# Two slots' value products in succession in a multi-head attention over 1024 tokens

## The chip, the cores and the metric
The kernel runs on one core of a Trainium2 chip. The metric is the device time in microseconds of one execution, as the median of several runs. One further execution was profiled; its rows give times in microseconds from the first instruction, durations of one instruction in nanoseconds in some views.

## The reference, cut to what matters
The program computes four layers on x (4 batches, 128 channels, 32 x 32 positions): two convolution-like blocks (a one-head attention, then a multi-head attention at three scales, fused), then two transformer layers on the 1024 tokens of each batch (causal one-head attention and 16 routed experts; 8-head attention with a bias and 8 experts). The change touches the 8-head attentions with 1024 tokens, of which there are two: scale 1 of the second block, and the attention of the last layer.

```python
attn = jnp.einsum('bhdn,bhdm->bhnm', q, k) / HEAD_DIM ** 0.5     # HEADS = 8, HEAD_DIM = 16
attn = jax.nn.softmax(attn, axis=-1)
out = jnp.einsum('bhnm,bhdm->bhdn', attn, v)
...
scores = jnp.einsum('bihd,bjhd->bhij', q, k) / jnp.sqrt(jnp.asarray(hd, x.dtype))
scores = scores + col_bias[None, :, None, :]
attn = jax.nn.softmax(scores, axis=-1)
out = jnp.einsum('bhij,bjhd->bihd', attn, v).reshape(B, N, D)
```

## The kernel before, in words
`many_heads_attention` is called for 1024, 256, 64 tokens (heads0, heads1, heads2) and once more for 1024 (heads3). The flag `whole` is true for 256 and 64 tokens. For 1024 tokens each of the 4 batches has 32 slots (`SLOTS`). A slot stands for one tile of 128 keys, against 512 queries, in 4 heads. Eight slots (`T`) make a chunk, two chunks (`NH`) make a half (4 of the 8 heads), two halves a batch. The first batch is written out, the others run in a loop whose body is the 32 slots, and a closing part runs the lag out.

All engines run over the same slots k, each with its own program, bound by semaphores:
- TensorE, first pass (`first_pass`, L777): two units per slot. A unit multiplies a tile of 128 queries with all 1024 keys, in two bf16 matmuls of 512 columns, into one of two banks `n_ps`.
- VectorE, `maximum` (L889): reduces a unit's 128 x 1024 scores to the negated maxima and so frees the bank (`first_used`). After eight slots it splits the maxima in bf16 parts (`rows_of`, L570 to L573). TensorE turns them in the next slot (`turn_maxima`, L784) through one of the same two banks, VectorE copies them out (L898), and SyncE writes them as extra rows of the queries (L710).
- TensorE, second pass (`second_pass`, L794), 10 slots later (`LAG`): the scores again, transposed and less the maxima, four matmuls (one per head) through three banks `t_ps`.
- ScalarE (L871): the exponential of each, into one of 8 buffers `prob`. Ahead of a group of four it waits that the mix two groups back is over (`mixed`).
- TensorE, `mix` (L806), one slot behind the second pass: the product with the values, four f32 matmuls, one per head, each with 32 columns of weights, so that the four heads use four column groups of the array; each matmul leaves two records. They add up in the bank `o_ps` over the eight slots of a chunk; VectorE copies it out (`keep_output`, L907).
- After the last chunk of a half, GpSimd sends the sums of the exponentials through DRAM, VectorE inverts them three slots later (`invert`, L936) and GpSimd multiplies the half with them (L850).

TensorE's order inside a slot is: first pass unit, second pass of heads 0 and 1, first pass unit, a turn where there is one, second pass of heads 2 and 3, mix. TensorE issues its matmuls in this order, so a wait of one holds up all behind it.

Of the kernel before, what the change touches and what calls it, by code (L numbers as in the profile page):

```python
# [61 lines left out]
def hold(eng, sem, value, held):  # L62

    eng.wait_ge(sem, value)
    eng.sem_inc(held, 1)
# [13 lines left out]
class Machine:  # L79
# [16 lines left out]
    def sb(self, name, shape, dt, ctx=None):  # L96
        return (ctx or self.ctx).enter_context(self.nc.sbuf_tensor(name, shape, dt))
# [478 lines left out]
def many_heads_attention(m, name, n, scratch, out, scale, bias_parts=None, ahead=None):  # L576
# [11 lines left out]
    TN, CH = min(P, n), min(512, n)  # L588
# [3 lines left out]
    whole = scratch.together  # L592
# [4 lines left out]
    R, SLOTS = UC // T, CPB * T  # L597
# [3 lines left out]
    assert NUSES % 2 == 0 and SLOTS * 4 % 8 == 0  # L601
    NROW = B * CPB if whole else CPB
    SUMS = 4 * n // P
    with Stage(nc) as ctx:
        sb = lambda nm, s, dt=F32: m.sb(f"{name}_{nm}", s, dt, ctx)
        qs, ks = (sb(x, [P, 8 * NBUF * n], BF16) for x in ("qs", "ks"))
        vs = sb("vs", [TN, B if whole else 1, T, 8 * SLOT])
        prob = [sb(f"prob{i}", [TN, CH]) for i in range(8)]
        mx, mrest, mparts = sb("mx", [TN, UC]), sb("mrest", [TN, UC]), sb("mparts", [TN, 3, UC], BF16)
        mrows = [sb(f"mrows{c}", [UC, 3, TN], BF16) for c in range(NROW)]  # L610
        if whole:
# [1 line left out]
        else:  # L613
            spread, inverse, wide = sb("spread", [P, SUMS]), sb("inverse", [P, SUMS]), [sb(f"wide{i}", [P, n]) for i in range(2)]
            sums_dram = nc.dram_tensor(f"{name}_sums_d", [4, n], F32, kind="Internal").ap()
# [9 lines left out]
        scored, exped, mixed, kept, dve_step = (m.sem(f"{name}_{x}", ctx) for x in ("scored", "exped", "mixed", "kept", "dve"))  # L625
# [8 lines left out]
        def query(b, rows, s, h, j, start, size):  # L634

            off = (((s * NH + h) * 4 + j) * NBUF + (b if whole else 0)) * CH + start
            return qs[rows, off:off + size]

        def key(b, rows, s, j, start, size):
            off = ((4 * s + j) * NBUF + (b if whole else 0)) * n + start  # L640
            return ks[rows, off:off + size]
# [8 lines left out]
        def over(b):  # L650
            return isinstance(b, int) and b == B

        def first_use(b):


            return (0, 0) if isinstance(b, int) and b == 0 else (b * NUSES - 1, 1)
# [12 lines left out]
        def score_bank(b, place, j):  # L669

            if whole:
                return (4 * (b * SLOTS + place) + j) % 3, 3
            q, per = 4 * place + j, 4 * SLOTS
            return q % 3, (3 if q >= 3 else per + q - max(x for x in range(per) if x % 3 == q % 3))
# [69 lines left out]
        @block.tensor  # L744
        def _(pe):
            if bias_parts is not None:
                pe.wait_ge(biased, 16)

            def wait(sem, value):

                if isinstance(value, int) and value <= 0:
                    return
                if TN < P:
                    hold(pe, sem, value, held_pe)
                else:
                    pe.wait_ge(sem, value)

            def emit(b, slots):
                done = first_use(b)
                uses = [0]  # L760

                def bank():

                    wait(first_used, done[0] + uses[0] - 1)
                    uses[0] += 1
                    return n_ps[(done[1] + uses[0] - 1) % 2]

                def first_pass(u):
                    c, j, t = u // UC, u % UC // TQ, u % TQ
                    s, h = c // NH, c % NH  # L770
                    if whole and u == 0:
                        wait(qk_loaded[b // LB], LOADS)
                    elif not whole and u % (NH * UC) == 0:
                        wait(qk_loaded[s], (b + 1) * LOADS)
                    ps = bank()
                    for i in range(NC):
                        last = pe.matmul(ps[0:TN, i * CH:(i + 1) * CH], query(b, slice(0, KB), s, h, j, t * TN, TN), key(b, slice(0, KB), s, j, i * CH, CH), start=True, stop=True)  # L777
                    last.then_inc(first_made, 1)

                def turn_maxima(of, c):  # L780
                    wait(rows_ready, of * CPB + c + 1)
                    ps = bank()[:].bitcast(BF16)
                    for part in range(3):
                        last = pe.transpose(ps[0:UC, part * TN:(part + 1) * TN], mparts[:, part, :], m.identb[0:TN, 0:TN])  # L784
                    last.then_inc(first_made, 1)

                def second_pass(of, place, heads):
                    c, t = place // T, place % T
                    if t == 0 and 0 in heads:
                        wait(row_loaded[of * CPB + c if whole else c], 48 * TQ if whole else (of + 1) * 48)  # L790
                    for j in heads:
                        i, back = score_bank(of, place, j)
                        wait(exped, 4 * (of * SLOTS + place) + j + 1 - back)
                        pe.matmul(t_ps[i][0:TN, 0:CH], key(of, slice(0, KM), c // NH, j, t * TN, TN), query(of, slice(0, KM), c // NH, c % NH, j, 0, CH), start=True, stop=True).then_inc(scored, 1)  # L794

                def mix(of, place):
                    c, t = place // T, place % T
                    s = c // NH
                    if place % (NH * T) == 0:
                        wait(v_loaded[of // LB if whole else s], 16 if whole else (of + 1) * 16)  # L800
                    if t == 0:
                        wait(kept, of * CPB + c)
                    wait(exped, 4 * (of * SLOTS + place + 1))
                    for j in range(4):
                        i = (4 * (of * SLOTS if whole else 0) + 4 * place + j) % 8
                        last = pe.matmul(o_ps[SLOT * j:SLOT * (j + 1), 0:CH], vs[:, of if whole else 0, t, (4 * s + j) * SLOT:(4 * s + j + 1) * SLOT], prob[i][:], start=(t == 0), stop=(t == T - 1))  # L806
                    last.then_inc(mixed, 1)

                for k in range(slots):
                    units = range(R * k, R * (k + 1)) if not over(b) else ()  # L810
                    of, place = behind(b, k, LAG)
                    for u in units[:R // 2]:
                        first_pass(u)
                    if of is not None:
                        second_pass(of, place, (0, 1))
                    for u in units[R // 2:]:
                        first_pass(u)
                    turned, at_ = behind(b, k, 1)
                    if at_ % T == T - 1 and turned is not None:
                        turn_maxima(turned, at_ // T)  # L820
                    if of is not None:
                        second_pass(of, place, (2, 3))
                    of, place = behind(b, k, LAG + 1)
                    if of is not None:
                        mix(of, place)

            over_batches(pe, emit)

        @block.gpsimd
        def _(pool):  # L830
# [6 lines left out]
            if not whole:  # L837
                def divide_half(b, s):
# [4 lines left out]
                    hold(pool, sums_out, (rounds + done) * 16, held)  # L843
                    pool.dma_start(spread[:], sums_dram.rearrange("h (c q) -> (h c) q", q=SUMS)).then_inc(sums_in, 16)
                    hold(pool, inverted, done, held)
                    pool.dma_start(inverse_dram.rearrange("h (c q) -> (h c) q", q=SUMS), inverse[:]).then_inc(inverse_out, 16)
                    hold(pool, inverse_out, (rounds + done) * 16, held)
# [10 lines left out]
        @block.scalar  # L858
        def _(act):
            def emit(b, slots):  # L860
                for k in range(slots):
                    of, place = behind(b, k, LAG)
                    if of is None:
                        continue
                    group = of * SLOTS + place
                    if not isinstance(group, int) or group >= 2:
                        act.wait_ge(mixed, group - 1)
                    for j in range(4):
                        act.wait_ge(scored, 4 * group + j + 1)
                        to = prob[(4 * (group if whole else place) + j) % 8]  # L870
                        act.activation(to[:], t_ps[score_bank(of, place, j)[0]][0:TN, 0:CH], ACT.Exp, scale=scale).then_inc(exped, 1)  # L871

            over_batches(act, emit)
# [1142 lines left out]
```

## Time and profile before

| | us |
|---|---|
| median of 3 runs | 2431.28 |
| lowest, highest | 2430.42, 2443.71 |
| span of the profiled execution | 2438.4 |
| own time of the profiled execution | not given apart; of the three runs only 2443.71 is longer than the span |
| busy in the span: TensorE, VectorE, ScalarE, GpSimd | 1686.4, 1549.6, 907.7, 321.6 |
| the two stages over 1024 tokens | from about 480 to 874 and from about 1780 to 2209 |

Busy time is the time in which at least one instruction of the engine runs. Matmul ends are modelled, so successive matmuls overlap in the rows; the difference of two starts says what a step takes.

### The profile page before, as it was taken

How to read it: one execution, taken by the hardware profiler on the slowest of the kernel's cores; microseconds unless marked ns; L12 is line 12 of the kernel's file. 1: busy time of each engine (PE TensorE's matmuls, PEld its weight loads, DVE VectorE, ACT ScalarE, POOL GpSimd, SP SyncE). 2: the span in 40 equal slices, each digit the busy share in tenths (PEclk: the TensorE clock that was granted, in tenths of full speed). 3: DMA queues.
4: the chain of work that ended last, by engine and by line, in shares of the span. 5: the costliest groups of instructions: out<-in, count | busy, mean ns of one | idle time of the engine just before them, and what ended most of it. 6: DMA issues, size and time to landing. Idle time of an engine off the chain costs nothing. (4 is left out here: it accounts for less than half of the span.)

```text
span 2438.4 us, 29945 instructions
## 1 busy us (share of the span) xinstructions
PE 1686.4 (69%) x8584; PEld 796.9 (33%) x8585; DVE 1549.6 (64%) x2931; ACT 907.7 (37%) x1695; POOL 321.6 (13%) x273
## 2 busy tenths in 40 slices
PE   5993232599999957578962059901569999895698
PEld 4772111122222212335632035600312222223476
DVE  4556987578878746445675534523668778775466
ACT  2331222166666623013330023301326666664143
POOL 0001532101000110001002720063010000110000
PEclk9996665599999975689975579955769999998699
DMA  1000131522224040103005432211442224200000
GB/s 40 0 0 6 43 129 52 80 35 55 45 49 66 28 69 3 42 1 133 0 1 164 138 84 66 75 51 27 175 69 46 45 50 65 47 28 0 18 0 35
DMA packets 123331, 125.68 MB, mean 52 GB/s; under 512 B 30867, under 2 KB 100955, under 8 KB 121323
## 3 DMA queue, kind: packets, MB, share of 16 engines
q1 hardware_dynamic: 104990, 101.91, 18.0%
q0 software_dynamic: 13088, 16.46, 2.3%
q10 hardware_dynamic: 5168, 6.29, 0.8%
q8 instruction: 39, 0.64, 0.1%
q14 instruction: 46, 0.38, 0.1%
HBM read 79.92 MB, written 44.22 MB: 51 GB/s over the span
## 5 line engine op out<-in xcount | busy, mean ns | idle before, releaser
L889 DVE TENSOR_REDUCE heads_mx<-heads_n_bank 128x1 f32<-128x1024 f32 (+2 forms) x608 | 631.9, 1081 | 180.3 <-PE heads_n_bank L777 177.4
L871 ACT ACTIVATE heads_prob<-heads_t_bank 128x512 f32<-128x512 f32 (+2 forms) x1120 | 559.1, 578 | 459.5 <-PE heads_t_bank L794 459.2
L777 PE MATMUL heads_n_bank<-heads_ks,heads_qs 96*128 96x512 bf16 (+3 forms) x1120 | 361.1, 403 | 135.4 <-DMA heads_ks<-scale_k_parts 56.1
L794 PE MATMUL heads_t_bank<-heads_qs,heads_ks 99*128 99x512 bf16 (+3 forms) x1120 | 341.1, 385 | 10.0 <-ACT heads_prob L871 7.4
L806 PE MATMUL heads_o_bank<-heads_prob,heads_vs 128*32 128x512 f32 (+2 forms) x2240 | 299.7, 610 | 4.1 <-issue 1.8
L777 PEld LDWEIGHTS heads_n_bank<-heads_ks,heads_qs 96*128 96x128 bf16 (+2 forms) x1120 | 88.6, 100 | 455.9 <-issue 173.7
L794 PEld LDWEIGHTS heads_t_bank<-heads_qs,heads_ks 99*128 99x128 bf16 (+2 forms) x1120 | 107.4, 101 | 208.8 <-ACT heads_prob L871 105.9
L1108 PE MATMUL in_p_bank<-in_src,in_wqk 128*128 128x512 f32 (+1 forms) x76 | 48.1, 792 | 171.2 <-DVE in_src L1126 130.4
L345 PE MATMUL attn_s_bank<-attn_k,attn_q 128*128 128x512 f32 x256 | 123.7, 612 | 0.0
L360 PEld LDWEIGHTS attn_o_bank<-attn_v,attn_probT 128*128 128x128 f32 x800 | 97.7, 192 | 47.1 <-ACT attn_probT L406 25.4
L360 PE MATMUL attn_o_bank<-attn_v,attn_probT 128*128 128x128 f32 x800 | 102.6, 279 | 8.4 <-ACT attn_probT L406 5.0
L260 PE MATMUL ln_ps_bank<-ident,ln_xn 128*128 128x128 f32 x64 | 17.5, 429 | 120.7 <-DVE ln_xn L240 65.3
L1725 DVE SCALAR_TENSOR_TENSOR x_channels<-experts_o_bank,combine,x_channels 128x128 f32 (+1 forms) x256 | 72.1, 344 | 41.7 <-PE experts_o_bank L1681 40.6
L1621 DVE TENSOR_TENSOR experts_hid<-experts_gate,experts_hp_bank 128x256 f32<-128x256 f32 x80 | 33.7, 421 | 99.9 <-ACT experts_gate L1601 98.4
L1560 PE MATMUL experts_hp_bank<-expert_w,experts_xT 128*128 x160 | 89.8, 643 | 7.0 <-DVE experts_hid L1621 3.2
L205 POOL DMA_INDIRECT ln_got<-routed_y,pick_slots x64 | 61.1, 954 | 193.1 <-issue 193.1
L1108 PEld LDWEIGHTS in_p_bank<-in_src,in_wqk 128*128 128x128 f32 x76 | 19.1, 266 | 195.8 <-issue 159.6
L1055 POOL TENSOR_TENSOR in_shared<-in_shared,in_product 128x1024 f32<-128x1024 f32 (+2 forms) x24 | 76.9, 3206 | 44.6 <-ACT in_product L1069 41.3
L1126 DVE SCALAR_TENSOR_TENSOR in_tap_sums<-padded,taps,in_tap_sums 128x1024 f32<-128x1024 f32 (+2 forms) x42 | 79.4, 1890 | 0.7
L1681 PEld LDWEIGHTS experts_o_bank<-experts_w,experts_hid 128*128 128x128 f32 x512 | 66.7, 193 | 29.9 <-issue 23.4
L806 PEld LDWEIGHTS heads_o_bank<-heads_prob,heads_vs 128*32 128x32 f32 (+1 forms) x2240 | 46.1, 112 | 82.4 <-issue 76.3
L1700 ACT ACTIVATE experts_hid<-experts_h_bank,experts_b 128x512 f32<-128x512 f32 x64 | 44.0, 688 | 72.8 <-PE experts_h_bank L1687 72.8
(263 smaller groups left out, 2223.2 us busy)
## 6 DMA issues: line engine op xcount, KB each, us to landing
edges_text<-edges_targets SPq DMA_DIRECT2D x4, 2048.0 KB
heads_qs<-scale_q_parts SPq DMA_DIRECT2D x60, 128.0 KB, 4.6
heads_ks<-scale_k_parts SPq DMA_DIRECT2D x60, 128.0 KB, 7.0
routed_x<-attn_zeros SPq DMA_DIRECT2D x3, 2560.0 KB, 13.2
experts_xs<-routed_x SPq DMA_DIRECT2D x24, 320.0 KB, 3.3
heads_wide<-heads_inverse_d POOLq DMA_DIRECT2D x14, 512.0 KB, 7.9
heads_qs<-edge_q_parts SPq DMA_DIRECT2D x48, 128.0 KB, 4.4
heads_ks<-edge_k_parts SPq DMA_DIRECT2D x48, 128.0 KB, 6.6
```

Source lines behind the costliest of these rows:

```text
L345: last = pe.matmul(s_ps[t % 2][:, h * 512:(h + 1) * 512], q[:, t * P:(t + 1) * P], k[:, h * 512:(h + 1) * 512], start=True, stop=True)
L360: last = pe.matmul(o_ps[:, 0:C], probT[t % 2][:, j, :], v[:, j, :], start=(j == 0), stop=(j == n - 1))
L777: last = pe.matmul(ps[0:TN, i * CH:(i + 1) * CH], query(b, slice(0, KB), s, h, j, t * TN, TN), key(b, slice(0, KB), s, j, i * CH, CH), sta ...
L794: pe.matmul(t_ps[i][0:TN, 0:CH], key(of, slice(0, KM), c // NH, j, t * TN, TN), query(of, slice(0, KM), c // NH, c % NH, j, 0, CH), start= ...
L806: last = pe.matmul(o_ps[SLOT * j:SLOT * (j + 1), 0:CH], vs[:, of if whole else 0, t, (4 * s + j) * SLOT:(4 * s + j + 1) * SLOT], prob[i][: ...
L871: act.activation(to[:], t_ps[score_bank(of, place, j)[0]][0:TN, 0:CH], ACT.Exp, scale=scale).then_inc(exped, 1)
L889: dve.tensor_reduce(mx[:, u % UC:u % UC + 1], bank()[0:TN, 0:n], AX.X, ALU.max, negate=True).then_inc(first_used, 1)
L1055: pool.tensor_tensor(image(shared), image(shared), image(product[i % 2]), ALU.add).then_inc(shared_added, 1)
L1108: pe.matmul(qk_ps[i][:, c * CH:(c + 1) * CH], wqk[:, i, :], chunk(c), start=True, stop=True).then_inc(qk_made, 1)
L1126: dve.scalar_tensor_tensor(out=image(sums if i < 8 else src), in0=window(b, i), scalar=weight, in1=image(sums), op0=ALU.mult, op1=ALU.add) ...
L1560: pe.matmul(h_ps[j % 2][:], xT[j % 2][:], w12[:, bass.ds(expert, 1), :].rearrange("p o h -> p (o h)"), start=True, stop=True).then_inc(ope ...
L1725: last = dve.scalar_tensor_tensor(out=tile, in0=o_ps[e % 2][:, t * P:(t + 1) * P], scalar=weight, in1=tile, op0=ALU.mult, op1=ALU.add)
```

## The change
For 1024 tokens a factor MIX = 2 is introduced (1 for the others). TensorE leaves out `mix` in the slots whose mixed place is even, and in the next slot does the mixes of both places, one behind the other. There are 16 probability buffers for 8, and ScalarE waits for the mix of four groups back. Each matmul stays as it is, and so does the order of everything else.

```diff
+    MIX = 1 if whole else 2
-        prob = [sb(f"prob{i}", [TN, CH]) for i in range(8)]
+        prob = [sb(f"prob{i}", [TN, CH]) for i in range(8 * MIX)]
...
-                        i = (4 * (of * SLOTS if whole else 0) + 4 * place + j) % 8
+                        i = (4 * (of * SLOTS if whole else 0) + 4 * place + j) % (8 * MIX)
...
                     of, place = behind(b, k, LAG + 1)
-                    if of is not None:
-                        mix(of, place)
+                    if of is not None and place % MIX == MIX - 1:
+                        for together in range(place - MIX + 1, place + 1):
+                            mix(of, together)
...
-                    if not isinstance(group, int) or group >= 2:
-                        act.wait_ge(mixed, group - 1)
+                    if not isinstance(group, int) or group >= 2 * MIX:
+                        act.wait_ge(mixed, group - 2 * MIX + 1)
...
-                        to = prob[(4 * (group if whole else place) + j) % 8]
+                        to = prob[(4 * (group if whole else place) + j) % (8 * MIX)]
```

## Rows read from the trace of the kernel before

**Rows 1.** The page, part 1: busy time, share of the span, instructions.
```profile
PE 1686.4 (69%) x8584; PEld 796.9 (33%) x8585; DVE 1549.6 (64%) x2931; ACT 907.7 (37%) x1695; POOL 321.6 (13%) x273
```
**Rows 2.** Windows of both stages: length, busy (x) by engine, clock, DMA share, GB/s.
```profile
480.00:874.00 394.00, 366.46 (x2033) 104.94 (x2029) 302.95 (x334) 262.93 (x506) 33.55 (x35) 0.98 0.24 43
1780.00:2209.00 429.00, 396.66 (x2096) 111.06 (x2096) 332.26 (x362) 266.51 (x512) 33.51 (x35) 0.94 0.26 45
```
**Rows 3.** Timeline, a plain slot: start, length, engine, line, operation, count [idle before <-releaser].
```profile
705.43 0.60 PE L777 MATMUL heads_n_bank<-heads_ks,heads_qs 96*128 96x512 bf16 x2
...
706.08 2.36 DVE L889 TENSOR_REDUCE heads_mx<-heads_n_bank 128x1 f32<-128x1024 f32 x2 [0.48 <-PE heads_n_bank L777]
...
706.31 0.60 PE L777 MATMUL heads_n_bank<-heads_ks,heads_qs 96*128 96x512 bf16 x2
...
706.74 0.59 PE L794 MATMUL heads_t_bank<-heads_qs,heads_ks 99*128 99x512 bf16 x2
...
707.27 0.64 PE L806 MATMUL heads_o_bank<-heads_prob,heads_vs 128*32 128x512 f32 x4
...
707.72 0.61 PE L806 MATMUL heads_o_bank<-heads_prob,heads_vs 128*32 128x512 f32 x4
...
708.27 0.60 PE L777 MATMUL heads_n_bank<-heads_ks,heads_qs 96*128 96x512 bf16 x2
...
708.51 0.69 DVE L907 COPY scale_out<-heads_o_bank 128x512 f32 x1
...
709.12 1.21 DVE L889 TENSOR_REDUCE heads_mx<-heads_n_bank 128x1 f32<-128x1024 f32 x1
```
**Rows 4.** Timeline, from the slot ahead of a turn to the slot after it.
```profile
719.60 0.60 PE L777 MATMUL heads_n_bank<-heads_ks,heads_qs 96*128 96x512 bf16 x2
...
723.56 2.35 DVE L889 TENSOR_REDUCE heads_mx<-heads_n_bank 128x1 f32<-128x1024 f32 x2
...
724.83 0.33 PE L784 MATMUL heads_n_bank<-identb,heads_mparts 128*16 128x128 bf16 x3 [0.93 <-DVE heads_mx L889]
...
726.63 0.60 PE L777 MATMUL heads_n_bank<-heads_ks,heads_qs 96*128 96x512 bf16 x2
```
**Rows 5.** Timeline, a stall and what follows it, VectorE and TensorE.
```profile
692.79 0.35 DVE L936 RECIPROCAL heads_inverse<-heads_spread 128x32 f32<-128x32 f32 x1 [3.69 <-DMA heads_spread<-heads_sums_d]
693.06 4.64 DVE L889 TENSOR_REDUCE heads_mx<-heads_n_bank 128x1 f32<-128x1024 f32 x4
...
694.27 0.61 PE L777 MATMUL heads_n_bank<-heads_ks,heads_qs 96*128 96x512 bf16 x2 [2.45 <-DVE heads_mx L889]
...
702.60 0.60 PE L777 MATMUL heads_n_bank<-heads_ks,heads_qs 96*128 96x512 bf16 x2
```
**Rows 6.** TensorE's waits, first stage, then second: us in total, times, longest.
```profile
PE heads_n_bank L777 <- DVE heads_mx L889: 10.6, 6, 2.4
...
PE heads_n_bank L777 <- DVE heads_mx L889: 11.5, 5, 2.5
```
**Rows 7.** Two idle stretches in the timeline, and windows with the clock behind each.
```profile
750.96 0.33 PE L784 MATMUL heads_n_bank<-identb,heads_mparts 128*16 128x128 bf16 x3 [1.46 <-DVE heads_mx L889]
...
2025.55 0.60 PE L777 MATMUL heads_n_bank<-heads_ks,heads_qs 99*128 99x512 bf16 x2 [1.87 <-DVE heads_mx L889]
...
750.90:754.30 3.40, 3.34 (x21) 1.08 (x21) 2.20 (x3) 1.77 (x4) 0.00 (x0) 1.00 0.20 77
...
2026.40:2029.80 3.40, 3.38 (x13) 0.64 (x12) 3.26 (x7) 2.17 (x4) 0.70 (x1) 0.50 0.16 19
```
**Rows 8.** Timeline, two slots at the end of the first stage.
```profile
868.86 0.82 PE L794 MATMUL heads_t_bank<-heads_qs,heads_ks 99*128 99x512 bf16 x3
...
871.32 0.82 PE L794 MATMUL heads_t_bank<-heads_qs,heads_ks 99*128 99x512 bf16 x3
...
871.81 2.06 ACT L871 ACTIVATE heads_prob<-heads_t_bank 128x512 f32<-128x512 f32 x4 [0.39 <-PE heads_t_bank L794]
...
872.46 0.39 PE L794 MATMUL heads_t_bank<-heads_qs,heads_ks 99*128 99x512 bf16 x1 [0.32 <-ACT heads_prob L871]
```

## The prediction
> **What bounds the kernel now.** First the page's busy shares: TensorE is busy in 69% of the span, VectorE in 64%, so neither bounds the whole and the answer is local [rows 1]. The table by windows puts the two head attentions over 1024 tokens at about 394 and 429 us; in both TensorE is busy for over 92%, VectorE for 77%, ScalarE for 62 to 67%, and the granted clock is 0.98 and 0.94 [rows 2]. The others (256 and 64 tokens) have MIX = 1 and stay as they are.
>
> The timeline of a plain slot [rows 3] shows TensorE as the bound: maxima pair u0 at 705.43, scores, maxima pair u1 at 706.31, scores at 706.74, mix at 707.27, next slot at 708.27. That is 2.84 us, 1.00 of it from the mix's start to the next matmul, and 0.53 from the last scores' start to the mix, against the usual 0.43: some 0.10 us of switch. VectorE works 2.36 us and waits 0.48, ScalarE works 2.06 (four of the 0.52 us in [rows 8]). So VectorE has 17% to spare, no more, and it depends on TensorE through only two maxima banks: u2 can't start before the reduction of u0 is over.
>
> Two places are not like that. Every eighth slot has a turn of the maxima, for which TensorE waits 0.93 us on VectorE [rows 4]: there VectorE is the bound. And at the third slot after each half's last output copy, VectorE waits for a DMA (the sums on their way through DRAM), 3.69 us in the case shown, and TensorE behind it for 2.45 us [rows 5]. Such a stall holds TensorE up 6 times in the first stage, for 10.6 us in all, and 5 times in the second, for 11.5 [rows 6].
>
> **The change, part by part.** Slots are counted by k within a batch. A mix now stands only in even slots, two together; odd slots have 1.75 us of TensorE work, less than VectorE's 2.36.
>
> *What is saved.* The second mix of a pair should need no switch. Its price from the rows: the second round of four records starts 0.45 us after the first (707.27, 707.72), so two rounds cost 0.90 us more, instead of 1.00 + 0.10. Below it could be 0.86 (two rounds at 0.43, the spacing of two bf16 pairs), above 1.09 (nothing saved). I take 0.90, nearest to the rows that show rounds in succession. Saved: 0.19 per pair.
>
> *What it costs in a plain pair.* Walk from u0 of the odd slot at 0, by [rows 3]: the reduction starts at 0.65; one alone takes 1.21, two together 2.36 (1.14 from start to start). It frees u0's bank at 1.87, and TensorE follows 0.06 later: u2 starts at 1.93, not at 1.75. The second reduction ends at 3.00: u3 starts at 3.06, not 2.81. From a slot's second maxima pair to its mix is 0.96 (706.31 to 707.27): mixes at 4.02, then 1.00 + 0.90: the pair ends at 5.92. Before: 5.67. **Plain pair: +0.25 us.** VectorE finishes u3's reduction at 5.28 and idles, since both mixes now stand between it and its next matmul. ScalarE doesn't bind: the eighth exponential ends near 5.1, each score bank is free (three banks, 0.52 us per exponential) before its matmul is due, and those of both mixed slots are a slot old. With 16 buffers its wait on a mix is met a slot early. Plain pairs outside the stalls: three per half (slots 1-2, 5-6, 9-10) in 14 halves, and seven at the ends and in halves without a stall: 49 x 0.25 = **+12.3**.
>
> *Pairs after an output copy* (slots 3-4): the copy (708.51 in [rows 3]) starts the reductions 0.2 us later (709.12 for 708.92). Hidden before, in the new order it delays u2 and u3. 17 x 0.46 = **+7.8**.
>
> *Pairs with a turn.* Before, from the slot ahead of the turn at 719.60: turn at 724.83, next slot at 726.63, 7.03 in all [rows 4]. The turn waits for VectorE's chain (two reductions, four small operations, the next slot's first reduction from 723.56), which doesn't start sooner in the new order; a mix that stood under this wait now stands behind it. **+0.90 each**, for 14 turns in mid-half and 3 at half ends without a stall: **+15.3**.
>
> *Stalled stretches.* The stall is tied to the copy at the end of slot 10 or 26 (the sums start there), and four slots fit into it. The new order loses 0.46 + 0.25 there, the stalls hold TensorE for 1.8 and 2.3 us on the mean [rows 6]: hidden, **0**. Behind it four reductions in a row (4.64 us) and a turn set the pace: 4.64, the four small operations 0.96, the next reduction 1.28, and from the turn to the next slot 1.80 (726.63 - 724.83), with the second mix 0.90 more: 9.58 us. Before, it was 9.54 in the case shown (702.60 - 693.06 [rows 5]), since the mix ahead of the turn had delayed it. **0**; where that mix didn't delay it, up to +0.5 each, where a clock at half rate did, less than nothing: within 3 us over the 11. The sums' DMA also shares queues with the next loads, which start when the scores of slot 9 or 25 are done, now 0.25 us earlier against the copy: between 0 and -2.7, I take **-1.4**.
>
> *End of each stage*, ten slots without maxima, 2.46 us each [rows 8]. TensorE waits at the fourth score matmul for a bank, the first exponential (0.49 behind the scores) being just over. Two slots in succession: the eighth score matmul waits for the fifth exponential, at 3.20; mixes at 3.52, end 5.42 for 4.92: +0.50, three such pairs. A turn and a DMA wait before them add 0.90 once. The last slot stays as it is, its mix waits for the exponentials in any order. 2 x (1.5 + 0.9) = **+4.8**.
>
> *Clock.* In [rows 7] an idle stretch of 1.46 us before a turn left the clock at 1.00, one of 1.87 was followed by 3.4 us at 0.50 (1.2 GHz). The new order's idle time before a turn is 1.57 (u3 over at about 3.66, turn at 5.23): between the two. Half rate over 3.4 us loses 1.7 us of matmul work, of which the slack of a next odd slot hides up to 0.3. Of some 29 turns I take three or four: **+5**, bounds 0 and +45. The Trainium skill ("TensorE: Matmul & The Clock Gate", "What's actually happening") says that the clock gate opens with activity and closes without it; the rows agree. It speaks against the change, since the work is bunched and idle time with it; it gives no price for this pattern.
>
> Sum: 12.3 + 7.8 + 15.3 + 0 - 1.4 + 4.8 + 5 = **+43.8 us**. The span is 2438.4, and of the three runs only 2443.71 can hold it, 5.3 more than the span: it would become 2487.5, span 2482.2. The median of the runs is 2431.28, so the forecast is **2475 us**. The eight more buffers cost memory, no time.
>
> **The rivals.**
> *The switch decides (faster).* If u2 and u3 never waited, 0.19 x 123 pairs = 23 us would be gained: 2408. It decides from the point where a reduction takes under 1.05 us; it takes 1.21, and both banks are needed. For it: VectorE's 0.48 us of idle time per slot. Against: that lies behind the mixes, and moves with them. 5%. The Trainium skill ("TensorEngine Tiling (Array Packing)", "Key Properties") has the rule behind this: a change of tiling mode drains TensorE, and the change halves these. The 0.10 us ahead of the mix agrees with it.
> *The stalls take it all.* If the inversion's DMA came earlier by as much as the pairs lose, and turns were relaxed by it: within 10 us, 2436. The turns in mid-half speak against it. 4%.
> *The clock halves at most turns.* 25 x 1.5 instead of 5: 2508. 12%.
> *Nothing is saved at the second mix* (1.09): 0.19 more at about 93 pairs off the stalls, +18: 2493. 12%. That would be the change not doing what it says.
> *Forecast:* 67%, its own range 2455 to 2490.
>
> The 8-in-10 range is 2450 to 2498: low, 2456 by the bounds of second mix (0.86, -4), DMA (-1.3), stalls (-3), clock (-5) and a smaller wait at u3 (0.1 us, -6), with some of the two fast rivals; high, the dearer second mix and some of the clock's. What a measurement can't tell from no change is 0.5%, 12 us. Faster by more: 5%; within: 4%; slower: 91%.
>
> **What would show it.** In the timeline: odd slots of about 1.93 us, even ones near 3.99, sum 5.92; two groups of eight L806 records 0.90 apart; VectorE idle for 1.2 us once per pair; turn waits of about 1.57 us; the slot before and with a turn 7.93 together; stalls after slots 10 and 26 shorter, with their next slot as long after the copy as before. Wrong if pairs take under 5.67, if u3 doesn't wait, or if stretches of half clock at turns decide.

## The result, and the profile after

The changed kernel takes 2504.31 us (median of 4 runs, 2498.66 to 2505.98), beside 2433.32 for the kernel before in the same session: ratio 1.0276, 95% interval 1.0246 to 1.0307, so 2.8% slower, 60 to 75 us. The forecast was 2475 with a range up to 2498. The direction was right; the size was not, and the time lies outside the range. The profiled execution has a span of 2496.8 us for 2438.4, and it is the fastest of the four of the changed kernel, while the one before is longer than its median: so the traces show 58.4 us of the 71.0 between the medians.

The page of the changed kernel, parts 1 and 5, beside [rows 1]:

```profile
PE 1717.7 (69%) x8584; PEld 805.2 (32%) x8585; DVE 1541.9 (62%) x2931; ACT 907.9 (36%) x1695; POOL 322.3 (13%) x273
...
L807 PE MATMUL heads_o_bank<-heads_prob,heads_vs 128*32 128x512 f32 (+2 forms) x2240 | 291.0, 638 | 4.1 <-issue 1.6
```

The same instructions. TensorE is busy for 31 us more, with the same matmuls, so some of them ran slower; the rest of the 58 us is waiting. The page does not show where. The timeline does. Here is TensorE in the changed kernel over a pair behind an output copy (559.02), a plain pair (565.12) and a pair with a turn (571.00), with VectorE's reductions of the plain pair (the changed file's lines are one or two higher: L778 first pass, L795 second pass, L785 turn, L807 mix, L891 reduction):

```profile
559.02 0.60 PE L778 MATMUL heads_n_bank<-heads_ks,heads_qs 96*128 96x512 bf16 x2
...
565.12 0.61 PE L778 MATMUL heads_n_bank<-heads_ks,heads_qs 96*128 96x512 bf16 x2
...
565.99 0.60 PE L778 MATMUL heads_n_bank<-heads_ks,heads_qs 96*128 96x512 bf16 x2
...
567.04 0.60 PE L778 MATMUL heads_n_bank<-heads_ks,heads_qs 96*128 96x512 bf16 x2
...
568.17 0.60 PE L778 MATMUL heads_n_bank<-heads_ks,heads_qs 96*128 96x512 bf16 x2
...
569.14 1.92 PE L807 MATMUL heads_o_bank<-heads_prob,heads_vs 128*32 128x512 f32 x16
571.00 0.60 PE L778 MATMUL heads_n_bank<-heads_ks,heads_qs 96*128 96x512 bf16 x2
...
574.05 0.61 PE L778 MATMUL heads_n_bank<-heads_ks,heads_qs 96*128 96x512 bf16 x2
576.24 0.49 PE L785 MATMUL heads_n_bank<-identb,heads_mparts 128*16 128x128 bf16 x3 [1.58 <-DVE heads_mx L891]
576.66 1.03 PE L795 MATMUL heads_t_bank<-heads_qs,heads_ks 99*128 99x512 bf16 x2
577.62 2.85 PE L807 MATMUL heads_o_bank<-heads_prob,heads_vs 128*32 128x512 f32 x16
580.41 0.60 PE L778 MATMUL heads_n_bank<-heads_ks,heads_qs 96*128 96x512 bf16 x2
```
```profile
565.76 4.62 DVE L891 TENSOR_REDUCE heads_mx<-heads_n_bank 128x1 f32<-128x1024 f32 x4 [1.26 <-PE heads_n_bank L778]
```

The plain pair goes as the forecast walked it. u2 starts 1.92 after u0 (567.04 - 565.12), u3 at 3.05, the mixes at 4.02; two of them take 1.86 to the next matmul (569.14 to 571.00), the second one 0.86; the pair is 5.88, and two plain slots before were 5.67 [rows 3]. VectorE works four reductions in a row and waits 1.26 us once per pair.

The pair with the turn is another matter. TensorE waits 1.58 us (0.93 in [rows 4]), and then the matmuls are slow: the second pass takes 1.03 where it took 0.60, the mixes 2.85 for 1.92. From 571.00 to 580.41 are 9.41 us; 7.93 was forecast at full clock. The windows ahead of and behind the turn say why (length, busy by engine, clock, DMA share, GB/s):

```profile
572.00:575.40 3.40, 2.55 (x11) 0.61 (x8) 3.14 (x7) 2.90 (x6) 0.00 (x0) 1.00 0.00 0
576.30:579.70 3.40, 3.40 (x17) 0.87 (x21) 1.27 (x2) 1.08 (x2) 0.00 (x0) 0.52 0.01 2
```

The clock stands at half rate, 1.2 GHz for 2.4, for the 3.4 us in which TensorE does the turn and most of its two mixes. This happens at 19 of the 30 turns behind the first mix: the clock record of the trace has 19 half-rate stretches in the two stages, 71.7 us in all, where the kernel before had 9 with 34.1 us, all of those at stalls. TensorE's waits in the two stages of the changed kernel, in the form of [rows 6], first the first stage, then the second:

```profile
PE heads_n_bank L785 <- DVE heads_mx L891: 23.2, 14, 2.1
PE heads_n_bank L778 <- DVE heads_mx L891: 8.3, 18, 1.4
```
```profile
PE heads_n_bank L785 <- DVE heads_mx L891: 23.2, 14, 2.1
PE heads_n_bank L778 <- DVE heads_mx L891: 4.5, 15, 0.8
```

The stalls behind the inversions (L778) have shrunk, as forecast; the turns (L785) wait 1.66 us on the mean.

### The profile page after: what moved, and what is told of

It reads as the page before. It is cut to its first block and busy times, and to the rows that moved or that the text cites. A ratio compares the mean times of both kernels' runs of the same rounds, so it can differ in the third digit from the quotient of the medians.

```text
span 2496.8 us, 29971 instructions
## 1 busy us (share of the span) xinstructions
PE 1717.7 (69%) x8584; PEld 805.2 (32%) x8585; DVE 1541.9 (62%) x2931; ACT 907.9 (36%) x1695; POOL 322.3 (13%) x273
## 5 line engine op out<-in xcount | busy, mean ns | idle before, releaser
L891 DVE TENSOR_REDUCE heads_mx<-heads_n_bank 128x1 f32<-128x1024 f32 (+2 forms) x608 | 624.3, 1080 | 231.9 <-PE heads_n_bank L778 226.0
L778 PE MATMUL heads_n_bank<-heads_ks,heads_qs 96*128 96x512 bf16 (+3 forms) x1120 | 359.3, 401 | 136.5 <-DMA heads_ks<-scale_k_parts 54.3
L795 PE MATMUL heads_t_bank<-heads_qs,heads_ks 99*128 99x512 bf16 (+3 forms) x1120 | 343.9, 385 | 13.4 <-ACT heads_prob L873 5.4
L807 PE MATMUL heads_o_bank<-heads_prob,heads_vs 128*32 128x512 f32 (+2 forms) x2240 | 291.0, 638 | 4.1 <-issue 1.6
L778 PEld LDWEIGHTS heads_n_bank<-heads_ks,heads_qs 96*128 96x128 bf16 (+2 forms) x1120 | 80.0, 100 | 414.5 <-DVE heads_mx L891 242.9
L795 PEld LDWEIGHTS heads_t_bank<-heads_qs,heads_ks 99*128 99x128 bf16 (+2 forms) x1120 | 107.6, 101 | 203.3 <-ACT heads_prob L873 100.6
L807 PEld LDWEIGHTS heads_o_bank<-heads_prob,heads_vs 128*32 128x32 f32 (+1 forms) x2240 | 61.7, 117 | 154.9 <-issue 115.0
```

The costliest lines, as they stand in the source:

```text
L891: dve.tensor_reduce(mx[:, u % UC:u % UC + 1], bank()[0:TN, 0:n], AX.X, ALU.max, negate=True).then_inc(first_used, 1)
```

## The experiments

Two theories were set against each other. **Order:** the loss is VectorE's two banks and the mix moved behind VectorE's chain. **Clock:** a large part is the half rate that follows the longer wait at a turn. Each ratio below is to the kernel before on the same chip, with its 95% interval. Chips differ: the kernel before took 2437, 2413, 2436 and 2412 us in the four sessions, so ratios are compared, not times. "Mid-half turns" are the 14 turns at slots 8 and 24 once mixes run, which no stall disturbs. A trace is one execution, and the number of half-rate stretches differs between executions.

**1. Filling the wait.** Zero weights on a tile of ones, added to the output bank: same results, but TensorE is busy.

```diff
                     if at_ % T == T - 1 and turned is not None:
+                        if not whole and behind(b, k, LAG + 1)[0] is not None and not over(b):
+                            for _ in range(6):
+                                pe.matmul(o_ps[:, 0:CH], blank[:], ones[:, 0:CH], start=False, stop=False)
                         turn_maxima(turned, at_ // T)
```

> The changed kernel; ahead of each turn of the maxima TensorE runs six bf16 matmuls of zero weights that add nothing to the output bank (1.3 us that fit under the wait). Clock theory: about half of the loss comes from TensorE's idle wait at the turn, after which the clock is granted at half rate; with the wait filled, the half-rate stretches behind turns go, the slot ahead of a turn and the turn's slot take 7.9 us together for 9.4, and the whole about 2480 against 2504. Order theory (all of the loss is in the order of mixes and VectorE's waits): no change, 2500 to 2506.

> As the kernel with six filling matmuls, but three (0.64 us), so that about 1.0 us of idle time is left at a turn, as much as the kernel before had. Clock theory: as with six, 2480, if the length of the idle stretch decides; if any bunching of waits decides, the half-rate stretches stay and so does 2504.

Six: 2474.24 us, ratio 1.0160 (1.0136 to 1.0185). Three: 2472.15 us, 1.0154 (1.0128 to 1.0181). Work added, some 30 us gained. In the trace with three (L781 first pass, L788 turn, L810 mix, L826 filling; the first filling matmul has no record):

```profile
567.26 0.61 PE L781 MATMUL heads_n_bank<-heads_ks,heads_qs 96*128 96x512 bf16 x2
...
570.31 0.60 PE L781 MATMUL heads_n_bank<-heads_ks,heads_qs 96*128 96x512 bf16 x2
570.97 0.59 PE L826 MATMUL heads_o_bank<-heads_ones,heads_blank 128*128 128x512 bf16 x2
572.49 0.33 PE L788 MATMUL heads_n_bank<-identb,heads_mparts 128*16 128x128 bf16 x3 [0.93 <-DVE heads_mx L900]
...
573.29 1.92 PE L810 MATMUL heads_o_bank<-heads_prob,heads_vs 128*32 128x512 f32 x16
575.15 0.60 PE L781 MATMUL heads_n_bank<-heads_ks,heads_qs 96*128 96x512 bf16 x2
```

The pair takes 7.89 us for 9.41, the mixes 1.92 again, and no half-rate stretch is left in either stage. The turn itself comes no sooner after u0 (5.23 us here, 5.24 in the changed kernel): VectorE sets it. By the ratios the half rate is worth 1.2%, about 30 us, and what is left against the kernel before is 1.5 to 1.6%.

What is left is not the order's whole price, since the kernel before has half-rate stretches of its own and the one with three filling matmuls has none. From the start of the first mix to the end of the last, the two stages together take 791.7 us before (34.1 at half rate), 814.9 with three filling matmuls (none) and 847.9 in the changed kernel (71.7). The last two differ by 33.0 us, or 0.46 us for each us at half rate. By this price the kernel before would be some 16 us shorter at full clock. So, as an estimate, the order costs 39 us, and the clock 33, of which 16 had been there before.

**2. How long a wait it takes.** First the opposite experiment: the kernel before, its order untouched, with VectorE made to split the maxima later.

```diff
                     dve.wait_ge(first_used, done[0] + uses[0])
+                    if not whole:
+                        for i in range(6):
+                            dve.tensor_copy(spare[:, i], mx[:])
                     split_in_three(...)
```

> The kernel before, mixes as they were; VectorE does six more copies of 16 columns (about 0.1 us each) ahead of splitting the maxima, so that TensorE's idle wait at each mid-half turn grows from 0.93 to about 1.5 us. If the length of the idle stretch ahead of a turn decides about the clock, half-rate stretches appear behind many turns: 0.6 x 29 = 17 us by the delay itself and up to 1.5 x 20 = 30 more by the clock, 2460 to 2485. If it takes the new order (odd slots without a mix), no such stretches: 2450 to 2455.

> The kernel before, order untouched, nine extra copies for six: TensorE's idle wait at mid-half turns should be 1.62 us, for 1.39 with six (where no mid-half turn was followed by half rate) and 1.58 in the changed kernel (where 19 of 30 turns were). If the idle length decides, half-rate stretches now stand behind more than half of the mid-half turns, and the time grows by 0.23 x 29 = 7 us over the one with six copies and 15 to 25 us more by the clock: 2450 to 2465 on a chip where before is 2433. If it takes the pairing, mid-half turns stay at full rate: about 1% over before.

> The kernel before with eight copies: 1.54 us of idle time at mid-half turns, no wait ahead of it. Between six (1.39 us, none of the mid-half turns followed by half rate) and nine (1.62 us, most of them). If the length of the single wait is what counts, some of the turns are followed by half rate and the time is 1.009 to 1.013 of before; with none, 1.009.

Six copies: 1.0067 (1.0049 to 1.0086), that is 16 us, the delay of 0.46 us at some 30 turns and little more. Nine: 1.0140 (1.0118 to 1.0161). Eight: 1.0135 (1.0111 to 1.0159), above the 1.009 to 1.013 expected. With nine, a turn and the window behind it:

```profile
574.08 0.33 PE L785 MATMUL heads_n_bank<-identb,heads_mparts 128*16 128x128 bf16 x3 [1.63 <-DVE heads_mx L890]
...
574.88 1.28 PE L807 MATMUL heads_o_bank<-heads_prob,heads_vs 128*32 128x512 f32 x8
576.10 1.04 PE L778 MATMUL heads_n_bank<-heads_ks,heads_qs 96*128 96x512 bf16 x2
```
```profile
575.60:579.00 3.40, 3.40 (x11) 1.04 (x8) 1.35 (x2) 1.34 (x3) 0.00 (x0) 0.50 0.02 4
```

With six, at the same place, the wait is 1.39 us and the next first pass runs at full rate:

```profile
575.62 0.33 PE L785 MATMUL heads_n_bank<-identb,heads_mparts 128*16 128x128 bf16 x3 [1.39 <-DVE heads_mx L890]
...
577.41 0.60 PE L778 MATMUL heads_n_bank<-heads_ks,heads_qs 96*128 96x512 bf16 x2
577.86 0.60 PE L795 MATMUL heads_t_bank<-heads_qs,heads_ks 99*128 99x512 bf16 x2
```

So the half rate doesn't need the pairing: a longer single wait is enough. Then the changed kernel with less filling:

> The changed kernel with one filling matmul per turn: idle stretch 1.58 - 0.21 = 1.37 us. If the idle length decides, with 1.39 not followed by half rate in the other order, nearly all half-rate stretches behind mid-half turns go, and the time is that of the kernels with three and six: 1.016 of before. If the half-rate stretches stay, it is the pairing: 1.027.

> The changed kernel with two filling matmuls per turn, 1.15 us of idle time left. With one (1.36 us) 16 half-rate stretches stayed and 1.024 of before, with three (0.93) none and 1.015. If a wait's length together with the short waits for u2 and u3 ahead of it decides, this lies near the three: at most 5 stretches, 1.015 to 1.018. If the first filling matmul (which left no record) had not run in time, this one equals the kernel with one: 1.023 or more.

One: 2496.71 us, 1.0239 (1.0216 to 1.0262). Two: 2457.82 us, 1.0186 (1.0164 to 1.0208), with three half-rate stretches in all, none at a mid-half turn. All together, counted in the clock record of each trace:

| kernel | wait at a mid-half turn | short waits ahead of it | followed by half rate |
|---|---|---|---|
| before | 0.93 us | none | 0 of 14 |
| before, 6 copies | 1.39 | none | 0 of 14 |
| before, 8 copies | 1.54 (1.49 at the first in each stage) | none | 2 of 14 |
| before, 9 copies | 1.63 | none | 10 of 14 |
| changed, 3 and 6 filling | 0.93, 0.28 | u2, u3 | 0 of 14 |
| changed, 2 filling | 1.15 | u2, u3 | 0 of 14 |
| changed, 1 filling | 1.58 in the rows, 1.36 if the matmul without a record ran | u2, u3 | 9 of 14 |
| changed | 1.58 | u2, u3 | 10 of 14 |

The counts for eight and nine copies bracket the change only roughly. The traced execution with eight took 2433.03 us, the other three 2440 to 2448 at a lower mean clock (0.817 to 0.821 for 0.823), so by that they had more half rate; the one with nine took 2480.60, the other three 2469 to 2472 at 0.817 to 0.819 for 0.813.

The expectation that one filling matmul would do, since 1.39 us had done no harm in the old order, was wrong. Two matmuls leave 1.15 us (1.58 less two of 0.21), so the one without a record did run there, and by that with one only 1.36 were left; yet 9 turns of 14 went to half rate. In the paired order a shorter wait is enough. The short waits for u2 and u3 (0.18 and 0.25 us), just ahead of it, are the difference at hand; that they count was not tried by itself.

**3. The mix ahead of the turn.** In a slot with a turn, the mix goes under TensorE's wait, in the kernel before and in the changed one.

```diff
+                    early = turning and not whole
+                    if early and behind(b, k, LAG + 1)[0] is not None:
+                        mix(*behind(b, k, LAG + 1))
                     if turning:
                         turn_maxima(turned, at_ // T)
...
-                    if of is not None:
+                    if of is not None and not early:
                         mix(of, place)
```

> The kernel before with one thing moved: in a slot with a turn, the mix stands ahead of the turn, under TensorE's wait for VectorE, and not at the slot's end. If a mix behind a turn costs its full 1.0 us because VectorE bounds there, this gains 0.9 at each of 14 turns in mid-half and at some of the others: 2433 becomes 2410 to 2420. Rival (the turn's later use is what bounds): within 5 us of before.

> The changed kernel with the two mixes ahead of the turn in slots with one. They take 1.9 us, the wait is 1.57 to 2.0, so the wait is filled with real work: no half-rate stretches behind turns and no mix behind the wait. Expected 2504 - 24 (clock) - 28 (1.6 us at 17 turns) = 2452, plain pairs staying at 5.89 us. If only the clock mattered, 2480; if neither, 2504.

The kernel before with it: 2415.40 us, ratio 0.9916 (0.9892 to 0.9940), faster than both kernels. The changed one with it: 2465.00 us, 1.0125 (1.0101 to 1.0151). TensorE in the first, around a turn at 720.36 that waits for nothing:

```profile
719.35 1.06 PE L806 MATMUL heads_o_bank<-heads_prob,heads_vs 128*32 128x512 f32 x8
720.36 0.33 PE L784 MATMUL heads_n_bank<-identb,heads_mparts 128*16 128x128 bf16 x3
720.62 0.60 PE L794 MATMUL heads_t_bank<-heads_qs,heads_ks 99*128 99x512 bf16 x2
721.49 0.60 PE L777 MATMUL heads_n_bank<-heads_ks,heads_qs 96*128 96x512 bf16 x2 [0.26 <-DVE heads_mx L893]
```

So a mix behind a turn did cost its time. The slot with a turn takes 3.54 us for 4.20: 0.66 gained and not 0.9, as VectorE is now late for the next u0. The trace has 23.9 us at half rate for 34.1 before, so some of the 0.8% may be the clock's.

In the changed kernel the pair with a turn falls to 6.38 us, but the next one takes 6.59 for 5.88. It waits for the maxima rows, which are needed two slots after the turn:

```profile
573.29 0.60 PE L795 MATMUL heads_t_bank<-heads_qs,heads_ks 99*128 99x512 bf16 x2 [0.81 <-DMA heads_qs<-heads_mrows]
```

Such waits come to 29.6 us in the two stages, at 29 places, for 3.6 us in the changed kernel. So at this turn 0.7 us was given back, and the ratio is 1.0125 where the expected 2452 would be 1.008.

**4. VectorE out of the way.** The maxima are taken of half the keys, in both orders; and the buffers alone.

```diff
-                    dve.tensor_reduce(mx[:, u % UC:u % UC + 1], bank()[0:TN, 0:n], AX.X, ALU.max, ...)
+                    dve.tensor_reduce(mx[:, u % UC:u % UC + 1], bank()[0:TN, 0:(n if whole else n // 2)], AX.X, ALU.max, ...)
```

> The kernel before with VectorE's reductions over 512 of the 1024 scores in the 1024-token stages (the maxima are taken of half the keys; the rest is computed as before). VectorE's plain-slot work falls from 2.36 to about 1.3 us. TensorE bounds plain slots as before, 2.83 us; turns get shorter: 2433 becomes 2390 to 2410. It is the partner of the next run.

> The changed kernel with the same halved reductions. If u2 and u3 wait for VectorE because of the two banks, the wait is gone and the saved switch shows: a pair takes 5.67 - 0.22 = 5.45 us, and this kernel is FASTER than its partner, by 0.2 us at some 120 pairs, 20 to 26 us. If a pair still takes 5.67 or more, the loss isn't VectorE's.

> The kernel before with 16 probability buffers and ScalarE's wait four groups back, mixes one per slot as before. ScalarE's wait for a mix never bound, so no change: within 3 us of before. If memory places or the looser wait mattered, more than that.

Order before: 2396.89 us, ratio 0.9932 (0.9910 to 0.9954). Changed order: 2431.63 us, 1.0078 (1.0056 to 1.0100), so 35 us slower than its partner and not 20 to 26 faster. The buffers: 0.9993 (0.9977 to 1.0009), nothing. The changed order with halved reductions, a plain pair from 726.93:

```profile
726.93 0.60 PE L778 MATMUL heads_n_bank<-heads_ks,heads_qs 96*128 96x512 bf16 x2
...
728.68 0.59 PE L778 MATMUL heads_n_bank<-heads_ks,heads_qs 96*128 96x512 bf16 x2
728.93 0.10 PEld L795 LDWEIGHTS heads_t_bank<-heads_qs,heads_ks 99*128 99x128 bf16 x1 [0.15 <-ACT heads_prob L873]
...
729.42 0.10 PEld L795 LDWEIGHTS heads_t_bank<-heads_qs,heads_ks 99*128 99x128 bf16 x1 [0.40 <-ACT heads_prob L873]
...
729.65 0.60 PE L778 MATMUL heads_n_bank<-heads_ks,heads_qs 96*128 96x512 bf16 x2
```

u2 now starts at 1.75: the two banks did hold it. But a pair takes 5.65 us (the next one starts at 732.58), only 0.02 less than two slots before: ScalarE and its three score banks take over, 0.1 us at u3 and 0.1 ahead of the mixes. So the 0.2 us that the forecast's fast rival counted on aren't there. That a pair gains nothing doesn't make it slower, though. TensorE's waits in the first stage, changed order, then the order before:

```profile
PE heads_t_bank L795 <- DMA heads_qs<-heads_mrows: 17.1, 7, 3.3
PE heads_n_bank L785 <- DVE heads_mx L891: 8.7, 13, 0.9
```
```profile
PE heads_t_bank L794 <- DMA heads_qs<-heads_mrows: 9.7, 7, 3.0
...
PE heads_n_bank L784 <- DVE heads_mx L889: 0.2, 1, 0.2
```

Over both stages the waits for the maxima rows' DMA are 34.3 us for 22.1, those at turns 17.9 for 0.5 (a mix that stood ahead of the turn now stands behind it), and the clock record has 54.6 us at half rate for 30.7. At 0.46 us each the last is some 11 us more. So three things carry the 35 us, as an estimate: 12, 17 and 11, less 3 at the stalls, 37 in all. None was tried by itself.

**5. The inversion two slots later,** to remove the stalls of [rows 5], alone and with the early mix.

```diff
-                        of, place = behind(b, k, LAG + 4)
+                        of, place = behind(b, k, LAG + 6)
...
-            emit(B, LAG + (1 if whole else 4))
+            emit(B, LAG + (1 if whole else 6))
```

> The kernel before with VectorE's inversion of the sums two slots later. The sums' DMA takes 12 us from the output copy in the stalled cases; five slots are 14 us, so the stalls behind 11 inversions (22 us of TensorE's waiting) mostly go. What is gained is less, as the loads for the next half could become the next wait: 8 to 20 us under before.

> The kernel before with both: mixes ahead of the turn in slots with one, and the inversion two slots later. If the two gains add up, 20 (as measured for the first, 0.8%) and that of the second: 1.5% under before. If the second is lost to another wait, 0.8 to 1.0% under.

Both are slower than the kernel before: 2484.66 us, 1.0206 (1.0176 to 1.0236), and 2480.37 us, 1.0171 (1.0151 to 1.0191). The stalls at L777 are gone, and the first stage has this in their place:

```profile
PE heads_t_bank L794 <- DMA heads_qs<-heads_mrows: 25.6, 6, 5.2
```

Two slots after a turn TensorE needs the maxima rows, whose DMA is issued on the queue that also carries the next half's loads. Without VectorE's stalls TensorE waits for these rows instead: 25.6 us for 10.6 in the first stage, 21.9 for 11.5 in the second. And the clock record has 68.3 us at half rate in the two stages for 34.1 before, at 0.46 us each some 16 us more. That the loads hold the rows up is the reading at hand; it was not tried by itself.

## Why the prediction was wrong

- *The order's terms held.* Second mix 0.90, measured 0.86. Plain pair 5.92, measured 5.88. Pair behind a copy 6.13, measured 6.10 (559.02 to 565.12). Pair with a turn at full clock 7.93, measured 7.89 (three filling matmuls). The wait at a turn 1.57, measured 1.58. VectorE's idle time per pair 1.2, measured 1.26. Without the clock the sum said 38.8 us; at full clock the order costs 39, by the estimate of experiment 1.
- *The step that failed is the clock's*: "Of some 29 turns I take three or four: +5". 19 half-rate stretches came, 10 of the 14 mid-half turns among them, and each costs 1.52 us (9.41 less 7.89); taken away, they give back about 30 us. The 9 stretches at stalls that the trace before has are gone, so there are ten more: 17 us in the traces (0.46 for each of 37.6 us) where +5 was put. The mechanism and the place were named, with the wait to 0.01 us, and so was the price of one (1.7 less up to 0.3). What failed is the choice between two rows, 1.46 without half rate and 1.87 with. The 1.57 was taken to be nearer to the harmless one. But the trace before has only one more wait of that kind (1.49 at 648.92, clock 1.00 behind it), two cases say little of a frequency, and the wait of 1.57 lies within 0.1 of the 1.63 at which the kernel with nine copies has half rate at 10 of 14 turns. The waits for u2 and u3 were left out of the comparison as well.
- *The rival with 12%,* the clock halving at most turns, gave 2508; 2504 was measured. That the two are so close is partly luck: it put 25 more stretches, and the traces have ten more. Of the miss of 29 us the traces show 14.6 (58.4 for 43.8), of which the clock has 12; 2 are the median before (2433.32 for 2431.28), and 12.6 lie between the traced executions and the medians (71.0 for 58.4), which no trace explains. Its chance and the upper end (2498) were too low. A threshold known only to lie between two rows, with the forecast between them, deserved something near even odds: 2475 and 2508 both belonged inside the range.
- *The other rivals fell.* Nothing saved at the second mix: 0.86 says no. The switch deciding: the point of 1.05 us per reduction and the 23 us were wrong, since ScalarE is the next bound and leaves 0.02 us per pair (experiment 4). The stalls taking it all: their waits shrank from 10.6 and 11.5 us to at most 8.3 and 4.5, but the turns in mid-half took far more.

## What to carry to other kernels

When work is bunched to save a switch, walk one period with the slack of every engine that shares buffers: here two banks let VectorE be ahead by two units only, and what was 17% slack per slot became a wait. Work behind a wait should go ahead of it, where the data allow: that alone makes the kernel before 0.8% faster. Look also at what the earlier work needs next: here it was the DMA of the maxima rows, which took back a part in experiments 3 to 5. An edit that lengthens TensorE's waits can have a second price in the clock, and where the traces only bracket its threshold, both outcomes belong in the range.

## What the runs showed of the hardware

- Waits far shorter than a half-rate stretch can bring one on: in the old order none of 14 at 1.39 us, 2 at 1.54, 10 at 1.63, in one execution each; a stretch lasts 3.4 us, a few 6.8. The Trainium skill ("TensorE: Matmul & The Clock Gate", "HAM oscillation — how this bites in real kernels") warns of long waits for DMAs between matmuls. The runs show that a single wait of 1.6 us for VectorE, once in some 25 us, can be enough.
- The stretches often follow each other at even distances: those in the changed kernel stand 27.3 us apart in rows (494.2, 521.5, 548.8, 576.1 in the first stage), and eight slots with one stretch are 27.2 to 27.3 us long (turn to turn, 493.1 to 520.3). Other turns with the same wait of 1.57 us are spared (605.2, 631.6). Why was not tried by itself.
- Two groups of four f32 matmuls of 32 weight columns in succession take 1.86 us to the next bf16 matmul, one group 1.00. So a group in succession costs 0.86, and the switch back, as an estimate from these two, about 0.14 us, beside the 0.10 ahead.
